# Last attention batch and early expert tiles: weight pieces in another order, their last low parts on VectorE, expert numbers loaded one by one, the third tile turned later

## The reference

```python
x = x + tanh(g_xattn) * attention(layernorm(x), ctx)        # argmax over scores, 16 heads, one shared key and value
logits = layernorm(x) @ gate_w                               # 8 experts
top_v, top_i = top_k(logits, 2); top_w = softmax(top_v)
for e in range(8):
    h = gelu(xf @ w1[e] + b1[e])                             # 256 -> 1024
    out += comb[:, e:e+1] * (h @ w2[e] + b2[e])              # 1024 -> 256
x = x + tanh(g_ffn) * out
```

## Time and profile before

| | us |
|---|---|
| median of 3 runs (912.28 to 915.21) | 912.65 |
| the profiled execution's own time | 919.3 |
| its span, first to last instruction | 917.4 |
| PE busy | 788.1 (86%) |
| DVE busy | 506.0 (55%) |
| POOL busy | 446.7 (49%) |
| ACT busy | 376.5 (41%) |

### The profile page before, as it was taken

One profiled execution on the slowest core, in us unless ns is written; L12 is line 12 of the kernel. 1 busy time (PEld: TensorE's weight loads), 2 busy tenths in 40 slices (PEclk: granted clock), 3 DMA queues, 4 the chain that ended last, 5 costly groups with the idle time before them and its releaser, 6 DMA issues.

```text
span 917.4 us, 19409 instructions
## 1 busy us (share of the span) xinstructions
PE 788.1 (86%) x6030; PEld 529.5 (58%) x6031; DVE 506.0 (55%) x1488; ACT 376.5 (41%) x788; POOL 446.7 (49%) x532
## 2 busy tenths in 40 slices
PE   2785789889797989887678889899999999999994
PEld 1332234334343434332257678789999989999773
DVE  3575676667667747676243874444554444444441
ACT  1222264635446463557562623233333333334231
POOL 4586472866667736464631763413343333333322
PEclk9877899999999999899798999999999999999998
DMA  5564332433543233323442333322233332222200
GB/s 173 123 132 137 59 116 36 161 83 116 111 127 95 69 117 76 94 72 125 153 144 76 65 100 72 56 43 47 44 55 51 50 49 46 46 42 36 43 12 2
DMA packets 63197, 74.64 MB, mean 81 GB/s; under 512 B 6800, under 2 KB 56848, under 8 KB 62992
## 3 DMA queue, kind: packets, MB, share of 16 engines
q1 hardware_dynamic: 49824, 56.74, 22.9%
q0 software_dynamic: 13296, 16.92, 10.4%
HBM read 46.75 MB, written 27.55 MB: 81 GB/s over the span
## 4 chain that ended last, share of the span: by engine, by line
PE 67%; DVE 9%; ACT 7%; issue 6%; POOL 5%; DMA 3%; SPq 1%; DVEq 1%; ACTq 0%; POOLq 0%
PE ps_o L2612 20%; PE ps_d L2596 9%; PE ps_a L2596 9%; PE ps_o L1345 6%; PE ps_d L1271 6%; PE ps_a L1334 3%; PE ps_e L1246 3%; PE ps_d L1313 3%; PE ps_e L1370 2%; PE ps_e L1229 2%; PE ps_r L2582 2%; DVE row_max L1031 2%; PE ps_r L1354 1%; POOL w_split L736 1%; ACT prob L846 1%
## 5 line engine op out<-in xcount | busy, mean ns | idle before, releaser
L2612 PE MATMUL ps_o<-w_split,hidden 128*128 x1136 | 192.4, 276 | 10.3 <-DVE y L2568 5.2
L846 ACT ACTIVATE prob<-ps_a 128x512 f32<-128x512 f32 x192 | 112.0, 603 | 172.5 <-PE ps_a L1334 171.7
L1031 DVE TENSOR_REDUCE row_max<-ps_d 128x2 f32<-128x384 f32 x237 | 127.6, 553 | 68.4 <-PE ps_d L1313 67.3
L2612 PE MATMUL ps_o<-w_split,h_lo 128*128 x568 | 156.6, 276 | 0.0
L2507 POOL DMA_INDIRECT out<-y,token_at x71 | 119.6, 1685 | 41.5 <-POOL token_at L2505 30.2
L2612 PEld LDWEIGHTS ps_o<-w_split,hidden 128*128 128x128 bf16 x1136 | 112.3, 99 | 27.0 <-issue 12.2
L2554 DVE TENSOR_TENSOR h_lo<-hidden 128x512 bf16<-128x512 f32 (+1 forms) x156 | 103.4, 698 | 32.2 <-ACT hidden L2523 31.5
L2568 DVE TENSOR_TENSOR y<-ps_o,b_all 128x512 f32<-128x512 f32 (+1 forms) x39 | 25.1, 643 | 153.2 <-PE ps_o L2612 144.7
L2596 PE MATMUL ps_a<-x_hi,w_split 128*128 128x256 bf16 (+1 forms) x624 | 105.7, 266 | 0.1
L2503 POOL TENSOR_TENSOR token_f<-tails,ones_f 128x2 f32<-128x2 f32 (+1 forms) x39 | 7.7, 196 | 200.9 <-DVE y L2571 198.6
L2596 PE MATMUL ps_d<-x_hi,w_split 128*128 128x256 bf16 (+1 forms) x624 | 104.7, 266 | 0.1
(11 more groups left out here) (250 smaller groups left out, 1255.5 us busy)
## 6 DMA issues: line engine op xcount, KB each, us to landing
w_stage<-w SPq DMA_DIRECT2D x32, 512.0 KB, 4.5
xg<-queue SPq DMA_DIRECT2D x31, 260.0 KB, 2.9
w_split<-q_split SPq DMA_DIRECT2D x48, 128.0 KB, 4.7
x_in<-x SPq DMA_DIRECT2D x8, 512.0 KB, 4.0
ctx_sb<-ctx_t SPq DMA_DIRECT2D x8, 512.0 KB, 3.9
x<-x SPq DMA_DIRECT2D x8, 512.0 KB, 4.3
q_split<-q_hl SPq DMA_DIRECT2D x16, 256.0 KB, 3.9
out<-x SPq DMA_DIRECT2D x8, 512.0 KB, 5.5
```

Source lines behind the costliest of these rows:

```text
L846: a.activation(prob[n % 2][:, j, :], ps_a[i % 2][:], ACT.Exp, scale=SCALE).then_inc(exp_ready, 1)
L1031: v.tensor_reduce(row_max[:, t, :, pair], bank[:, 0:2 * SLOTS].rearrange("p (h r) -> p h r", h=2), AX.X, ALU.max).then_inc(max_taken, 1)
L2612: last = nc.tensor.matmul(ps_y[:, t, :], hs[s][:, f, token], k.w2_split[:, bass.ds(e, 1), part, f, :].rearrange("p a d -> p (a d)"), start ...
```

## The change

The pieces are ordered by (expert, piece) pairs: behind experts 0 to 4 come the w2 pieces of experts 6 and 5, then their w1 pieces, then expert 7. Period 4 handles three pieces and period 5 four (two each before), period 6 three and period 7 two (four each before). The low parts of the last six pieces (from W_DVE = 26) are made by DVE instead of POOL: two in period 7, four in the end steps. The last four pieces stand at end steps 6, 11, 17, 19. PE loads only the number of expert 0 at step 20 and each further one in part 2 of layer 1 of the tile before it. Tile 2 is turned at end step 6 instead of 2 (`split_x` and `prepare` move along). The last sums are copied at end step 1 instead of 2, and the steps from the last batch's ratio to its queue slots stand one step later.

```diff
-        W_ORDER = (0, 1, 2, 3, 4, 6, 5, 7)
-        W_AT = {-2: (4, 10, 18, 26), -1: (4, 10, 18, 26), 6: (4, 10, 18, 26), 7: (2, 8, 14, 20)}
+        W_PIECES = (*((e, c) for e in range(5) for c in range(4)), (6, 2), (6, 3), (5, 2), (5, 3), (6, 0), (6, 1), (5, 0), (5, 1),
+                    *((7, c) for c in range(4)))
+        W_AT = {-2: (4, 10, 18, 26), -1: (4, 10, 18, 26), 4: (12, 14, 26), 5: (12, 14, 22, 26), 6: (4, 10, 18), 7: (4, 10)}
+        W_BATCHES = {(6, 0): 6, (6, 1): 6, (5, 0): 7, (5, 1): 7, **{(7, c): B for c in range(4)}}
+        W_DVE = 26
...
-        END_PIECES = (0, 12, 15, 18)
-        END_WEIGHTED, END_SUMS, END_TURN_SUMS, END_TAKE_HEADS = 1, 2, 3, 4
+        END_PIECES, END_TURN_TILE_2 = (6, 11, 17, 19), 6
+        END_WEIGHTED, END_SUMS, END_TURN_SUMS, END_TAKE_HEADS = 1, 1, 3, 4
...
-        END_CHOOSE, END_RATIO, END_RANK, END_SHARES, END_QUEUE = 20, 21, 22, 22, 23
+        END_CHOOSE, END_RATIO, END_RANK, END_SHARES, END_QUEUE = 20, 22, 23, 23, 24
...
+        def end_turned(step, layer, i, n):
+            if step == END_TURN_TILE_2:
+                return 2
+            return i + 1 if layer == 1 and n == 0 and 2 <= i < EARLY - 1 else None
...
                 for i in pieces(p, step, 1):
-                    piece_lo(i)
+                    if i < W_DVE:
+                        piece_lo(i)
...
-                if step - 1 in END_PIECES:
-                    piece_lo(N_PIECES - 4 + END_PIECES.index(step - 1))
...
+            def piece_lo(i):
+                if i == W_DVE:
+                    dve.wait_ge(w_lo, i)
+                dve.wait_ge(w_hi, i + 1)
+                hi, lo, stage = w_piece(i)
+                v.tensor_tensor(lo, stage, hi, ALU.subtract).then_inc(w_lo, 1)
...
+                tile = end_turned(step, layer, i, n)
+                if tile:
+                    k.prepare(dve, chain, tile)
                 if layer == 1:
-                    if n == 0 and i + 1 < EARLY:
-                        k.prepare(dve, chain, i + 1)
                     k.low(dve, i, n)
                 elif n == PAIRS - 1:
                     k.finish(dve, i)
+                if step - 1 in END_PIECES:
+                    piece_lo(N_PIECES - 4 + END_PIECES.index(step - 1))
...
-                    expert = [k.load_expert(pe, i) for i in range(EARLY_BATCHES)]
+                    expert = [k.load_expert(pe, 0)]
...
-                    if n == 0 and i + 1 < EARLY:
-                        turn_tile(i + 1)
+                    if n == PAIRS - 2 and i + 1 < EARLY:
+                        expert.append(k.load_expert(pe, i + 1))
...
                     if (i, n) == (EARLY_BATCHES, 0):
                         pe.wait_ge(w_lo, N_PIECES)
-                        expert += [k.load_expert(pe, more) for more in range(EARLY_BATCHES, EARLY)]
```

More of the change, by code:

```diff
@@ L464, in w_piece @@
         def w_piece(i):
-            e, c = W_ORDER[i // 4], i % 4
+            e, c = W_PIECES[i]
             stage = w_stage[i % 2][:]
@@ L887, in piece_hi @@
                 act.wait_ge(w_loaded[i % 2], 16 * (i // 2 + 1))
-                if i >= 20:
-                    act.wait_ge(logits_ready, LOGITS * (6 + (i - 20) // 4))
+                if W_PIECES[i] in W_BATCHES:
+                    act.wait_ge(logits_ready, LOGITS * W_BATCHES[W_PIECES[i]])
                 a.copy(hi, stage).then_inc(w_hi, 1)
@@ L942, in _ @@
                         k.gelu(act, 0, before)
+                tile = end_turned(step, layer, i, n)
+                if tile:
+                    k.split_x(act, tile)
                 if layer == 1:
-                    if n == 0 and i + 1 < EARLY:
-                        k.split_x(act, i + 1)
                     k.gelu(act, i, n)
@@ L1181, in _ @@
                     k.prepare(dve, chain, 0)
+                for i in pieces(p, step, 1):
+                    if i >= W_DVE:
+                        piece_lo(i)
             chain.restart()
@@ L1491, in _ @@
                     turn_tile(1)
+                tile = end_turned(step, layer, i, n)
+                if tile:
+                    turn_tile(tile)
                 if layer == 1:
-                    if n == 0 and i + 1 < EARLY:
-                        turn_tile(i + 1)
+                    if n == PAIRS - 2 and i + 1 < EARLY:
+                        expert.append(k.load_expert(pe, i + 1))
                     if i == 0:
```

## The result

The changed kernel takes 903.04 us in the median of four runs (900.67 to 904.71), the kernel before 913.07 beside it: a ratio of 0.9868, 95% interval 0.9837 to 0.9898. It is faster, by 10 to 12 us (12.0 against the 914.9 of a later comparison, at the same ratio). 897 had been forecast, with 892 to 905 as the range. The profiled executions lie further apart than the medians: 919.3 against 904.44, spans of 917.4 and 902.4, so 15.0 us, close to the 15.6 of the sum. Most of this document is about that difference.

A forecast was written before the change was run, and what follows sets the result against it. PE was taken as full from 600 us on, with time to gain around 447 to 485 us from waits, loads and low clock. Terms -6.6 - 9.2 - 0.5 + 0.7 = -15.6 took 912.65 to 897 us; range 892 to 905.

The forecast's parts named there:

- part 1: Period 7 up to the gates: 6.6 us less, from the piece stall and five of six loads going; bounds 3.4 and 7.5.
- part 2: End steps 0 to 10, to the turn of tile 3: 9.2 us less by shorter waits on DVE; bounds 4.6 and 10.3.
- The 1.2 of clock: Period 7 up to the gates: 1.2 us of PE clock won back, counted within the 6.6 us gain.
- the short gap of 0.6 at step 20: Expected sign in period 7: PE shows one short issue gap of 0.6 us instead of 3.48.
- PE's gaps ahead of layer 1 parts: Sign of being wrong: PE's gaps ahead of the layer 1 parts add up to more than 2 us.
- The walk of 15.73: End steps, first wait to turn of tile 3: 14.53 us of full-clock rows plus two waits, against 24.54 us before.
- Part 3: Turn of tile 3 to its layer 2: 0.5 us less; bounds 1.6 us less and 2.5 us longer.
- Part 4: Costs elsewhere: 0.7 us more, seven loads at 0.1 each; added casts and low parts in periods 4 and 5 taken as 0.
- the kept low clock: Rival, chance 0.12: waits go, but PE stays at its lower clock level through the same matmuls as before; 903 us.
- the long lows: Rival, chance 0.10: DVE's four low parts in the end steps take 2.75 us and more; 900 to 903 us.
- the replaced stall: Rival, chance 0.09: in period 7 PE arrives early at tile 0 or the rows and waits there; 903 us.
- the slower case: Rival, chance 0.04: longer wait ahead of tile 3's layer 2 leaves PE mostly at low clock, gates to tile 4; 918 us.

## Why the prediction was right, and where it was wrong

What the prediction said of each step is seen in the traces; the size was too large by 3.6 to 5.6 us, and the point lay 6 us below the median. In a table, from milestone to milestone, in us, the first trace of the changed kernel against the first two of the kernel before (the first is the one the sum was made on):

```
stretch                              forecast  1st trace  2nd trace
up to the gates of period 6             0        -0.9       -0.4
gates 6 to gates 7 (part 1)            -6.6      -6.6       -7.6
gates 7 to turn of tile 3 (part 2)     -9.2      -7.2       -1.4
turn of tile 3 to its layer 2 (3)      -0.5      -0.9       -0.9
from there to the end (4)              +0.7      +0.5       -0.5
sum                                   -15.6     -15.0      -10.8
```

Against the third trace of before part 2 is -8.8 and the sum -18.6. That the sum of the first trace came within 0.6 of the forecast is in part luck: part 2 fell short by 2.0, and 0.9 of what made up for it lies ahead of the gates of period 6, where nothing was forecast.

Part 1 held: 40.09 us between the gates became 33.53. Its split did not: the loads were put at 2.90 and are worth 4.75, as ACT stands still with PE and the clock falls behind the gap; the stall for the piece was put at 2.51 and is worth 2.86. Together that is the 7.6 of the second trace. The 1.2 of clock that I added most likely goes with the loads; no run shows it by itself. ACT has no wait for a weight piece left in period 7, as forecast, and of the short gap of 0.6 at step 20 no more than the 0.33 ahead of 450.15 is seen, which the trace puts on ACT. PE's gaps ahead of layer 1 parts, named as a sign of being wrong, come to 0.15 us up to 560 us.

Part 2 is the step that failed, at the sentence that `take_heads` waits behind a low of 2.75 us beside POOL and that this is most of the 2.96. The mechanism is right. The Trainium skill (SBUF — State Buffer, Who interferes with whom) says that a VectorE instruction with two SBUF inputs, as a low has, contends with a GpSimd instruction that reads SBUF; the runs agree, with 2.75, 2.98, 2.95 and 5.99 us for lows of 0.69, each ending about 0.6 us behind POOL's own end, though each began ahead of POOL's row (by 0.05 to 0.60 us; POOL's spans are rough). But it is a matter of 1 us which low is caught, and in the profiled execution the lower clock behind the wait for x_lo had moved the wrong one there. Its 1.99 us of wait and the lower clock behind the two waits, 5.8 of 36.94 us, are not in the second trace. So the prediction's reading that the lower level stands behind waits of 2.69 us and more is that of one trace: behind the 2.70 of the second it is the full one.

I then took the gain off the median although the profiled execution lay 6.65 us above it, and that distance was the very thing to explain. The other part of the miss is small: 1.6 us of clock behind the gates, at 457.89, in both traces of the changed kernel. Without it, in the kernel with the loads undone, the stretch is 27.85 us (489.23 - 461.38); forecast were 27.7. The walk of 15.73 was priced well: it is 16.04 in the changed kernel (486.87 - 470.83). Its upper bound, 10.3, is 10.45 by its own terms.

Part 3 held in size and in kind: the low parts at 1.22, tile 3's wait of 5 to 7 at 6.27, near 525, with DVE's tables behind it. The lower clock there costs 1.9 (7.18 us for 48 matmuls, 5.24 at full level), but the kernel before paid as much behind its 3.75 (7.09 us for its 48, from 540.96). Part 4 is not settled: from layer 2 of tile 3 to the end it is 0.5 us more than in the first trace of before and 0.5 less than in the second and third, and in periods 4 and 5, where the added casts and low parts stand, no loss is seen.

Of the rivals, the kept low clock came true at one place of 1.6 us, the long lows did not (the low parts take 1.22, the lows 0.69), the replaced stall did not, and the slower case did not: behind 6.27 us of waiting PE was back at full level after some 18 of 48 matmuls (1.94 us lost, at 0.11 for one matmul more). Against that case the prediction had said that PE kept twelve matmuls in 1.31 after most of the waits; in its own trace the first matmuls behind 2.69, 2.96, 2.99 and 3.75 all ran at the lower level. Three rivals named 903 or a range up to it, and 903.04 was measured, but none of the three came about as described. The forecast's own range, 892 to 902, does not hold it; that the wider one does is luck in so far as it was widened for these rivals.

## What to carry to other kernels

Before a gain is read off a profile, set the profiled execution beside the median: where it lies far above, look for a meeting of two engines that 1 us of phase would undo, take a second trace, and price the meeting by how often it comes. A register load on an engine that feeds a serial chain costs the whole chain its length and the clock behind it, so spread such loads behind queued work. A long table calculation on the vector engine is cheap if it is taken in pieces between the work that others wait for: that gave 5 to 7 us on top of the change.

## What was not expected of the hardware

The same wait is followed by either level of PE's clock, in one and the same kernel. Behind the wait for x_lo, 2.69, 2.70 and 2.71 us in the three traces of the kernel before, twelve matmuls take 2.57, 1.32 and 2.58. Behind the 2.02 us ahead of the gates they take 1.42, 1.42 and 2.55 there, 2.67 in both traces of the changed kernel, and 1.42 in both traces of it with tile 2 turned at end step 2. The kernel with the loads undone stood 3.72 us for issue some 8 us earlier and kept the full level behind the gates (1.42). The Trainium skill (TensorE: Matmul & The Clock Gate, What's actually happening) has activity lift the clock; these rows don't contradict it, but the length of the wait ahead does not tell which level follows. What does was not found, so a gain that rests on the level is worth what several traces show and not one.

The other surprise is how small an instruction can be and still be held up: 0.22 us of `is_choice` became 3.43 beside POOL's low part, while a low of 5.99 beside two of them cost next to nothing: DVE's next work, y of tile 1, had PE to wait for (5.08 us of idle DVE ahead of it in the changed kernel).
